# Eight matmul widths cut to three in TensorE's program of a routed expert layer

## The chip, the cores and the metric

The kernel runs on one core of a Trainium2 chip. The metric is the device time of one execution in microseconds (us), from the first to the last instruction and the little that lies around them. Lower is better.

## The reference, cut to what matters

```python
x = x + xattn(layernorm(x), ctx, W_k, b_k, gamma, beta)   # 4 x 1024 rows of 1024
xf = layernorm(x).reshape(4096, 1024)
probs = softmax(xf @ gate_w)                              # 8 experts
topk_w, topk_idx = top_k(probs, 2); topk_w /= topk_w.sum(-1)
# each row goes to its two experts; rows are sorted by expert:
h = silu(ragged_dot(rows, w1, sizes)) * ragged_dot(rows, w3, sizes)   # 1024 -> 3584
out = ragged_dot(h, w2, sizes)                                        # 3584 -> 1024
x = x + sum over the two experts of topk_w * out
```

All of it is float32. 8192 pairs of a row and an expert are spread over 8 experts, so an expert has about 1024 rows. How many is known only when the kernel runs.

## The kernel before, in words

A first part (the function `attend_and_route`, some 590 us) does the attention and the routing and leaves, for each expert, a list of its rows. Then `experts` works through slots. A slot is one expert with up to 1088 of its rows; this input fills eight slots, here called slot 0 to slot 7, one for each expert.

In a slot the rows lie in two halves side by side, so a matmul's moving side has as many columns as half the rows of the slot. That number, rounded up to one of the entries of `WIDTHS`, is the width of the slot. TensorE (PE) multiplies in the seven products of a Strassen scheme instead of eight, and each float32 operand is split into a high and a low part, so every product takes three matmuls for each k.

A slot has two stages. In the unit stage a unit is seven products of one weight (w1 or w3) for a pair of tiles of the hidden dimension: 28 units, each of 7 x 4 x 3 = 84 matmuls, or 168 where the width is over 512 and each matmul is cut in two. In the down stage there are seven passes over w2, each of five groups of steps, 168 matmuls (or 336) to a pass. Between the passes PE transposes: the rows of the next slot (`turn_rows`, L1789) or results on their way out (`turn_back`, L1808). ScalarE (ACT) makes the high parts of the weights and of the hidden rows, VectorE (DVE) the low parts and the sums (L1333 and L1336), and both empty PSUM. SyncE (SP) issues the loads of weights and the stores and loads of the hidden rows, which go through memory in `hd`. GpSimd (POOL) adds the results to the output by indirect DMA (`scatter`), and with `stage_pair` it loads w2 for sums (`stage`, the tiles `w2v` and `xg_0`).

All engines loop over the slots. ACT and DVE have three copies of a slot's code, for widths up to 512, 528 and 544. PE's loop over the units (L1824) and its loop over the groups (L1835) contain one body for every entry of `WIDTHS`; `by_width` (L1765) writes a binary search of compares and branches (L1772) around them, which is gone through again for each unit and each group. The bodies stand in the program from the widest to the narrowest. The engine's instructions are fetched from memory while it runs; the profile counts these fetches as packets of the queue q8 (16 KB each) and q14 (8 KB each).

In a unit PE waits at product 3 for ACT's copy of product 0's result (`s_s1`), at product 4 for DVE's sum u2 (`s_u2`, L1434), and at product 6 for DVE's c22 (`s_c22`, L1451). Ahead of c22, DVE has `down_sum(s, i, 0)` (L1450), which waits for the w2 that POOL's `stage_pair` loads:

```python
                if a == 0:
                    dve.wait_ge(s_sst, pr * 16 + 16)
                    down_sum(s, i, 0)
                plus(in_sbuf(to[:, 3], cols), in_sbuf(v, cols), in_psum(b4, cols)).then_inc(s_c22, 1)
```

In the down stage each group begins with `ready` (L1719), a wait for the low parts of w2 and of the hidden rows. The first of these hidden rows are loaded again only after SP has stored the last pair of the unit stage.

Of the kernel before, what the change touches and what calls it, by code (L numbers as in the profile page):

```python
# [61 lines left out]
SLOTS = 2 * T // (2 * HALF) + E - 1  # L62
META = 16
META_STEPS = 44
WIDTHS = (256, 384, 448, 480, 496, 512, 528, 544)
COLS = WIDTHS[-1]
TAIL = COLS - 4 * P
N8_MOST = COLS // 8
# [64 lines left out]
def attend_and_route(nc, x, ctx_in, W_k, b_k, gamma, beta, gate_w, x1_out, x2_rows, table, meta, first_weights):  # L133


    with ExitStack() as st:
# [440 lines left out]
        def _(dve):  # L577
# [175 lines left out]
            def by_slot(a):  # L753
# [30 lines left out]
            step(V.tensor_copy(metaf[:, 3, :], im[:, 1, :]))  # L784
            step(V.scalar_tensor_tensor(out=metaf[:, 2, :], in0=metaf[:, 3, :], scalar=float(WIDTHS[0] // 8),
                                        in1=has, op0=ALU.max, op1=ALU.mult))
# [85 lines left out]
def experts(nc, w1, w3, w2, out, x2_rows, table, meta, raw13, s_raw13):  # L872

    with ExitStack() as st:
# [229 lines left out]
        def _(act):  # L1104
# [179 lines left out]
            def slot(s, cols):  # L1284

                with act.Fori(0, PAIRS - 1) as i:
                    silu(free_at_start[:, 15:16], free_at_start[:, 14:15])
                    unit(s, i, 0, cols, lambda e: weight_hi(s, i, 1, e))
                    unit(s, i, 1, cols, lambda e: weight_hi(s, i + 1, 0, e))
                i = PAIRS - 1  # L1290
                silu(free_at_start[:, 15:16], free_at_start[:, 14:15])
                unit(s, i, 0, cols, lambda e: weight_hi(s, i, 1, e))

                def begin_down(e):
                    if e < 2:
                        w2_hi(s, e)
                    elif e in (3, 4):
                        h_hi(s, e - 3, cols)

                unit(s, i, 1, cols, begin_down)  # L1300
                down_phase(s, cols)
# [13 lines left out]
            with act.Fori(0, SLOTS) as s:  # L1315
                width = slot_value(act, 2, s, N8_MOST)
                with act.If(width > 0):
                    with act.If(width > BANK // 8):
                        with act.If(width > WIDTHS[-2] // 8):
                            slot(s, WIDTHS[-1])  # L1320
                        with act.Else():
                            slot(s, WIDTHS[-2])
                        act.nop()
# [5 lines left out]
        def _(dve):  # L1329
# [281 lines left out]
            def slot(s, cols):  # L1611

                with dve.Fori(0, PAIRS - 1) as i:
                    unit(s, i, 0, cols, lambda e: weight_lo(s, i, 1, e), lambda n: weight_sum(s, i, 1, n))
                    unit(s, i, 1, cols, lambda e: weight_lo(s, i + 1, 0, e), lambda n: weight_sum(s, i + 1, 0, n))
                i = PAIRS - 1
                unit(s, i, 0, cols, lambda e: weight_lo(s, i, 1, e), lambda n: weight_sum(s, i, 1, n))

                def begin_down(e):
                    if e < 2:  # L1620
                        w2_lo(s, e)
                    elif e in (3, 4):
                        h_lo(s, e - 3, cols)

                unit(s, i, 1, cols, begin_down, lambda n: None)
                down_phase(s, cols)
# [35 lines left out]
            with dve.Fori(0, SLOTS) as s:  # L1662
                width = slot_value(dve, 2, s, N8_MOST)
                with dve.If(width > 0):
                    with dve.If(width > BANK // 8):
                        with dve.If(width > WIDTHS[-2] // 8):
                            slot(s, WIDTHS[-1])
# [393 lines left out]
```

## Time and profile before

| what | value |
|---|---|
| time, three runs | 7847.52, 7869.36, 7878.46 us (median 7869.36) |
| time of the profiled execution | 7854.22 us |
| its span | 7852.5 us |
| PE busy | 7385.4 us, 94% of the span |
| DVE busy | 5046.7 us, 64% |
| ACT busy | 2873.4 us, 37% |
| POOL busy | 906.6 us, 12% |
| DMA | 159 GB/s over the span |
| granted clock of TensorE, mean | 0.97 |

The span is the time from the first to the last instruction. PE is busy nearly throughout, and 94% is a mean: in the middle of a unit stage it never stops, and between the stages it stands still for some microseconds. The chain of work that ended last has 85% of the span in PE, 3% in "issue" (an engine waited for nothing that the profile shows), 2% in DVE and 2% in DMA.

### The profile page before, as it was taken

What the parts mean: (1) busy time and instruction counts of PE and PEld (TensorE: products, weight loads), DVE (VectorE), ACT (ScalarE), POOL (GpSimd) and SP (SyncE); (2) the same over time, 40 slices, a digit from 0 to 9 for tenths busy, and PEclk for the clock granted to TensorE, in tenths of its full rate; (3) what the DMA queues carried; (4) which work ended last, traced back from release to release, by engine and by line L of the source; (5) the groups of instructions that cost most, each with busy time, mean ns of one, the idle gap of its engine ahead of it and who ended that gap; (6) DMA issues with size and microseconds to landing.
All of it is one profiled execution on the core that took longest, in us unless ns stands there. A gap on an engine that the chain in (4) does not pass through costs nothing.

```text
span 7852.5 us, 139132 instructions
## 1 busy us (share of the span) xinstructions
PE 7385.4 (94%) x45405; PEld 6600.8 (84%) x45406; DVE 5046.7 (64%) x8017; ACT 2873.4 (37%) x4875; POOL 906.6 (12%) x1344
## 2 busy tenths in 40 slices
PE   8959999899999999899999999999999999999998
PEld 5547877788779999888778999878778999999998
DVE  6767766577556665577556665577655665566655
ACT  2323334333443334333343333433343333433343
POOL 2330010100110010100010001100111001110011
PEclk8979999999999999999999999999999999999999
DMA  3333446544664445544564445544564445644455
GB/s 118 107 106 132 166 163 193 164 160 164 192 186 140 147 154 180 155 156 156 175 189 140 155 142 184 174 147 157 175 188 155 149 149 167 187 142 148 150 181 162
DMA packets 683970, 1247.95 MB, mean 159 GB/s; under 512 B 50528, under 2 KB 286448, under 8 KB 683632
## 3 DMA queue, kind: packets, MB, share of 16 engines
q1 hardware_dynamic: 584240, 935.24, 36.3%
q0 software_dynamic: 99392, 309.05, 12.2%
q8 instruction: 109, 1.79, 0.1%
q14 instruction: 229, 1.88, 0.1%
HBM read 840.81 MB, written 405.38 MB: 159 GB/s over the span
## 4 chain that ended last, share of the span: by engine, by line
PE 85%; issue 3%; DVE 2%; DMA 2%; ACT 0%; POOL 0%; SPq 0%; DVEq 0%; POOLq 0%; ACTq 0%
PE pair L1693 56%; PE pair L1726 27%; PE pair L1808 1%; DVE wl L1333 1%; DMA raw<-hd 1%; DMA raw<-in_L_ffn_w 1%; DVE sil L1336 0%; DVE hid L1336 0%; PE pair L1789 0%; DVE sil L1554 0%; ACT wh L1106 0%; DVE sil L1333 0%; POOL out_x L1926 0%; DVE xl L1333 0%; DVE hid L1424 0%
## 5 line engine op out<-in xcount | busy, mean ns | idle before, releaser
L1693 PE MATMUL pair<-xh,wh 128*128 128x264 f32 (+3 forms) x9408 | 2520.7, 322 | 100.5 <-issue 76.6
L1693 PE MATMUL pair<-xh,wl 128*128 128x264 f32 (+3 forms) x9408 | 2521.4, 323 | 12.9 <-issue 12.9
L1693 PE MATMUL pair<-xl,wh 128*128 128x264 f32 (+3 forms) x9408 | 2516.4, 322 | 0.0
L1333 DVE TENSOR_TENSOR wl<-raw,wh 128x512 fp32r<-128x512 f32 (+2 forms) x1875 | 1260.9, 692 | 1030.6 <-ACT wh L1106 1028.3
L1693 PEld LDWEIGHTS pair<-xh,wh 128*128 128x128 f32 x9408 | 1582.2, 190 | 240.7 <-issue 115.3
L1693 PEld LDWEIGHTS pair<-xh,wl 128*128 128x128 f32 x9408 | 1576.9, 189 | 141.7 <-issue 13.9
L1693 PEld LDWEIGHTS pair<-xl,wh 128*128 128x128 f32 x9408 | 1577.2, 189 | 122.4
L1106 ACT ACTIVATE wh<-raw 128x512 fp32r<-128x512 f32 (+2 forms) x1875 | 1136.9, 628 | 1351.3 <-PE pair L1693 611.8
L1726 PE MATMUL pair<-wh 128*128 128x264 f32 (+3 forms) x4704 | 1141.6, 326 | 144.4 <-issue 77.4
L1726 PE MATMUL pair<-wh,wl 128*128 128x264 f32 (+3 forms) x4704 | 1264.8, 323 | 0.0
L1726 PE MATMUL pair<-wl,wh 128*128 128x264 f32 (+3 forms) x4704 | 1264.5, 323 | 0.0
L1106 ACT ACTIVATE wh<-sums 128x512 fp32r<-128x512 f32 x900 | 566.3, 631 | 1545.2 <-PE pair L1693 1517.3
L1726 PEld LDWEIGHTS pair<-wh 128*128 128x128 f32 x4704 | 762.4, 191 | 231.7 <-issue 115.6
L1889 POOL TENSOR_TENSOR ticks<-ticks 128x1 f32<-128x1 f32 x316 | 115.9, 367 | 6333.5 <-DVE xg L1333 3276.3
L1726 PEld LDWEIGHTS pair<-wl,wh 128*128 128x128 f32 x4704 | 794.3, 191 | 62.8
L1726 PEld LDWEIGHTS pair<-wh,wl 128*128 128x128 f32 x4704 | 793.4, 191 | 63.1
L1333 DVE TENSOR_TENSOR wl<-sums,wh 128x512 fp32r<-128x512 f32 x900 | 616.8, 687 | 203.1 <-ACT wh L1106 195.0
L1336 DVE TENSOR_TENSOR part<-part,pair 128x512 f32<-128x512 f32 (+2 forms) x448 | 312.7, 698 | 469.6 <-PE pair L1693 469.6
L1333 DVE TENSOR_TENSOR wl<-part,wh 128x512 fp32r<-128x512 f32 (+1 forms) x272 | 186.5, 691 | 353.5 <-ACT wh L1106 353.1
L1106 ACT ACTIVATE wh<-part 128x512 fp32r<-128x512 f32 (+1 forms) x272 | 170.7, 630 | 421.1 <-PE pair L1726 397.8
L1109 ACT ACTIVATE sil<-sil 128x512 f32<-128x512 f32 (+2 forms) x336 | 215.5, 641 | 273.5 <-DVE sil L1336 262.3
L1336 DVE TENSOR_TENSOR sil<-part,pair 128x512 f32<-128x512 f32 (+2 forms) x368 | 254.8, 693 | 36.4 <-PE pair L1693 33.0
(253 smaller groups left out, 5473.4 us busy)
## 6 DMA issues: line engine op xcount, KB each, us to landing
raw<-in_L_ffn_w SPq DMA_DIRECT2D x226, 1024.0 KB, 7.8
raw<-hd SPq DMA_DIRECT2D x720, 272.0 KB, 3.6
hd<-hid SPq DMA_DIRECT2D x112, 1088.0 KB, 4.4
hd<-sil SPq DMA_DIRECT2D x112, 816.0 KB, 6.8
raw<-w2s SPq DMA_DIRECT2D x256, 256.0 KB, 3.3
w2v<-in_L_ffn_w POOLq DMA_DIRECT2D x112, 512.0 KB, 3.6
xg<-in_L_ffn_w POOLq DMA_DIRECT2D x112, 512.0 KB, 4.7
w2s<-w2v POOLq DMA_DIRECT2D x112, 512.0 KB, 5.2
```

What stands on the lines that cost most here:

```text
L1106: return nc.scalar.activation(out, in_, ACT.Copy)
L1109: return nc.scalar.activation(out, in_, ACT.Silu)
L1333: return V.tensor_tensor(out, a, b, ALU.subtract)
L1336: return V.tensor_tensor(out, a, b, ALU.add)
L1693: mm = pe.matmul(to[:, c, 0:hi - lo], entry(w, e)[:, ks], x[:, e, k, lo:hi], start=begin and k == 0 and i == 0, stop=k == KH - 1 and i == ...
L1726: mm = pe.matmul(pair[d][:, ch, 0:hi - lo], down_w(w, b)[:, d * P:(d + 1) * P], down_h(h, b)[:, lo:hi], start=begin, stop=end, skip_group_ ...
L1808: mm = pe.transpose(o, yT[:, d, j * P:j * P + r], ident[:, :])
L1889: G.tensor_tensor(ticks[:, 0:1], ticks[:, 0:1], ticks[:, 1:2], ALU.add).then_inc(s_tick, 1)
```

## The change

The list of widths loses five of its eight entries. The widest, 544, stays, and so do all sizes of buffers. What else is made from the list: the least value of a slot's stored width (L785, in eighths of a column, 32 before and 64 now), and PE's bodies and the search around them. A slot whose half has up to 512 columns now runs the body of 512; before, there were 256, 384, 448, 480 and 496 below it.

```diff
-WIDTHS = (256, 384, 448, 480, 496, 512, 528, 544)
+WIDTHS = (512, 528, 544)
```

PE's program has 1409 rows of different instructions before and 680 after. Those of DVE, ACT, POOL and SP are the same, in the same order.

At the head of the unit stage PE's order differs in the number of compares on the way to the first body in the program (the one of 544). The rows below are a piece of the difference; L1878 is the test for an empty slot, L1824 the entry of the loop over the units, L1698 and L1699 the first waits of a unit:

```order
 L1878 COMPARE_AND_BRANCH
 L1824 UNCONDITIONAL_BRANCH
-L1772 COMPARE_AND_BRANCH x3
+L1772 COMPARE_AND_BRANCH
 L1698 ISA
 L1699 ISA
```

The search has three levels before and one or two now; the first compare is against the same kind of register as before.

At the end of the loop over the units, just ahead of the down stage, PE's last body in the program before is that of 256 columns:

```order
L1693 MATMUL pair<-xh,wh 128x256
L1693 MATMUL pair<-xl,wh 128x256
L1693 MATMUL pair<-xh,wl 128x256
L1774 UNCONDITIONAL_BRANCH
L1824 REGISTER_ALU
L1824 COMPARE_AND_BRANCH
L1829 ISA
```

In the changed program the same place follows the body of 512 columns (`pair` is a PSUM tile, `xh` and `xl` the parts of the rows, `wh` and `wl` those of the weights):

```order
L1693 MATMUL pair<-xh,wh 128x512
L1693 MATMUL pair<-xl,wh 128x512
L1693 MATMUL pair<-xh,wl 128x512
L1774 UNCONDITIONAL_BRANCH
L1824 REGISTER_ALU
L1824 COMPARE_AND_BRANCH
L1829 ISA
```

Five bodies of 84 matmuls that stood between the body of 512 and the loop's end are gone, and the down stage, which follows, begins that much earlier in the program. In the loop over the groups five bodies of 40 matmuls are gone in the same way.

## Rows read from the trace of the kernel before

**Rows 1.** The page, its first line.
```profile
span 7852.5 us, 139132 instructions
```

**Rows 2.** Groups by line and form, L1693: count | busy us, mean ns | idle before.
```profile
L1693 PE MATMUL pair<-xh,wh 128*128 128x512 f32 x1568 | 620.3, 396 | 25.8 <-issue 21.3 <-DVE part L1336 2.6 <-ACT part L1106 1.8
L1693 PE MATMUL pair<-xh,wh 128*128 128x496 f32 x1568 | 613.0, 391 | 37.0 <-issue 17.9 <-DVE xl L1333 16.7 <-DVE wl L1333 2.4
```

**Rows 3.** The chain that ended last, in pieces: start us, us, what.
```profile
628.72 504.58 PE pair L1693 x2256
...
1331.04 38.01 PE pair L1726 x168
...
3298.32 524.19 PE pair L1693 x2256
...
4021.56 38.86 PE pair L1726 x168
```

**Rows 4.** Waits of PE from 600 us on: total us, times, longest us.
```profile
PE pair L1693 <- issue: 89.5, 17, 15.0
PE pair L1726 <- issue: 77.4, 25, 11.6
```

**Rows 5.** DMA queues, 1455 to 1500 and 5647 to 5702 us: packets, MB, share.
```profile
q8 instruction: 7, 0.11, 1.0%
...
q8 instruction: 5, 0.08, 0.5%
```

**Rows 6.** Timeline, turn from slot 5 to 6: start, us, instruction, [idle before].
```profile
5961.24 1.97 PE L1808 MATMUL pair<-ident,sil 128*128 128x128 f32 x16 [1.21 <-DVE sil L1336]
...
5969.81 0.58 PE L1693 MATMUL pair<-xh,wh 128*128 128x264 f32 x1 [6.61 <-issue]
...
5976.51 0.69 DVE L1333 TENSOR_TENSOR sums<-raw 128x512 f32<-128x512 f32 x1 [10.14 <-issue]
...
6001.10 0.80 PE L1693 MATMUL pair<-xh,wh 128*128 128x264 f32 x2 [3.34 <-issue]
```

**Rows 7.** Timeline, turn from slot 1 to slot 2.
```profile
2317.12 1.97 PE L1808 MATMUL pair<-ident,sil 128*128 128x128 f32 x16 [1.22 <-DVE sil L1336]
...
2342.64 0.69 DVE L1336 TENSOR_TENSOR xg<-w2v,xg 128x512 f32<-128x512 f32 x1 [1.15 <-DMA xg<-in_L_ffn_w]
...
2350.47 0.51 PE L1693 MATMUL pair<-xh,wh 128*128 128x272 f32 x2 [3.12 <-issue]
```

**Rows 8.** Chain in pieces, turns to slots 2 and 3, down stage of 3.
```profile
2344.10 3.28 PE pair L1693 x24
...
3285.48 10.20 PE pair L1693 x36
...
3844.55 0.69 DVE wl L1333
```

**Rows 9.** Timeline, turns to slot 3 and to slot 7.
```profile
3281.65 0.69 DVE L1333 TENSOR_TENSOR sums<-raw 128x512 f32<-128x512 f32 x1 [19.08 <-issue]
...
3298.32 0.49 PE L1693 MATMUL pair<-xh,wh 128*128 128x512 f32 x1 [2.67 <-issue]
...
6916.64 0.69 DVE L1333 TENSOR_TENSOR sums<-raw 128x512 f32<-128x512 f32 x1 [15.61 <-issue]
...
6935.02 0.66 PE L1693 MATMUL pair<-xh,wh 128*128 128x264 f32 x2 [2.88 <-issue]
```

**Rows 10.** Timeline of PE, start of the down stages of slots 3 and 5.
```profile
3826.93 1.09 PE L1789 MATMUL pair<-ident,xg 128*128 128x128 f32 x8 [1.64 <-DVE hid L1336]
...
3851.13 1.19 PE L1726 MATMUL pair<-wh 128*128 128x512 f32 x2 [11.42 <-issue]
...
3890.79 1.19 PE L1726 MATMUL pair<-wh 128*128 128x512 f32 x4 [1.13 <-DVE wl L1333]
...
5648.97 1.09 PE L1789 MATMUL pair<-ident,xg 128*128 128x128 f32 x8 [1.64 <-DVE hid L1336]
...
5701.69 1.19 PE L1726 MATMUL pair<-wh 128*128 128x512 f32 x4 [1.14 <-DVE wl L1333]
```

## The prediction, made before the changed kernel ran

> **What bounds the kernel now.** I read the page first: the span is 7852.5 us [rows 1], and PE is busy in 94% of it. Then the groups of matmuls kept apart by form, to learn which bodies this input uses. A slot issues 28 x 7 x 4 = 784 matmuls of xh with wh, so 1568 of 496 columns are two slots, and 1568 of 512 are two more [rows 2]. The other four slots run 528 (three) and 544 (one), in halves of 264 and 272. The bodies of 256, 384, 448 and 480 are never run. The chain in pieces tells which slots: 0 and 1 have 496 columns; 2 has 544; 3 and 5 have 512; 4, 6 and 7 have 528.
>
> So the change does two things to what runs. Slots 0 and 1 go from 496 to 512 columns, 16 more to each matmul, and those columns are waste. And PE's program gets about half as long, with one or two compares to find a body where there were three.
>
> In the middle of a unit stage PE is the bound without a gap. One piece of the chain holds 2256 matmuls in 504.58 us at 496 columns, another as many in 524.19 us at 512 [rows 3]. A compare costs nothing there, since PE's sequencer is ahead of its matmuls: I see no idle time at the seams of the units. The waits of PE show where it does stand: 89.5 us in 17 waits ahead of L1693 and 77.4 us in 25 waits ahead of L1726 that no semaphore explains [rows 4]. The timeline puts the long ones where PE goes from a slot's last transposes to the next slot's first unit, at the end of that first unit, and at the start of the down stage. Just there the queue q8 moves packets of 16 KB of instructions: 7 at the turn to slot 1, 5 at the start of the down stage of slot 5 [rows 5]. From 640 to 1130 us, 26 units long, the same view has no row for q8 at all. So PE keeps what a loop uses and fetches again when it goes to another part of the program.
>
> **The change, term by term.**
>
> *Columns.* 524.19 - 504.58 = 19.6 us for 2256 matmuls, 8.7 ns each [rows 3]. A slot's unit stage has 2352: +20.4 us, for two slots +40.8. A pass of the down stage takes 38.01 us at 496 and 38.86 at 512 [rows 3]: 0.85 x 7 = 6.0 a slot as the upper end. Some passes at 496 wait for DVE's halves, which hides part of it, so the lower end is nothing; I take 3.5 a slot. Sum of the columns: +47.8 us, from 40.8 to 52.8.
>
> *How much fits.* PE's code for a slot holds, before, 6 x 84 + 2 x 168 = 840 matmuls in unit bodies, 6 x 40 + 2 x 80 = 400 in group bodies and about 105 transposes, each with its weight load: 2690 instructions, with waits and branches some 3050. This code costs 7 + 5 = 12 packets in a slot [rows 5], so a packet is about 256 instructions. After the change it is 420 + 200 + 105 = 725 matmuls, 1450 instructions, some 1610 in all: 6.4 packets, so 7, and one more that is fetched ahead. Whether PE keeps 8 is the open point. The rows show that it keeps the 5 or 6 that the loop over the passes needs and does not keep 12. Eight is nearer to six than to twelve, so I take it that 8 fit; then PE fetches its slot code once, in slot 0, and never again.
>
> The Trainium skill bears on this (Runtime: NRT & Kernel Launch, Instruction fetch mechanics): PE's instruction memory is 128 KiB in blocks of 16 KiB, which makes 8 blocks and 2048 instructions. By it the sum stays as I make it, with all 8 places taken and none to spare. The same section says that a taken branch to a target outside a window of two pages forces a fetch. By that sentence alone nothing would be saved, as in rival 2. The trace speaks against it: each unit of 496 columns jumps over several bodies, and no packet moves.
>
> *What is late next at a turn.* Without the fetch PE would start the next slot within a microsecond of its last transposes. But ACT and DVE enter their own new code, which doesn't change, and POOL still has to scatter. Turn to slot 6: the transposes end at 5963.2, PE starts at 5969.8, DVE at 5976.5, and the second unit starts at 6001.1, 37.9 us after the transposes [rows 6]. Turn to slot 2, where PE's fetch was short: DVE has to wait for POOL's load of w2 until 2342.64, 23.55 us after the transposes [rows 7]; then comes c22, product 6 starts at 2344.10 and lasts 3.28 us [rows 8]. That is the floor, 28.3 us after the transposes, and after it come 3.1 us of fetch at the loop's end. So slot 2 gains 3.1 us. Slots 1, 4 and 6 look alike (within 1 us of it now, DVE in time); they fall to 28 each: 37.9 - 28 = 10, three times, -30 us.
>
> Where DVE is late it is the floor. At slot 3 it starts at 3281.65 [rows 9], and PE's product 4 starts 3.83 us after that; three products take 10.20 us [rows 8], though 36 x 0.232 = 8.4 at full rate: PE comes back slow from a stall. Only the fetch of 2.67 us at the end goes. At slot 7: 6916.64 + 3.8 + 10.6 = 6931.0 where 6935.02 is now [rows 9]: -4.0. Slot 5 is like slot 3, and I count 1. Sum of the turns: -3.1 - 30 - 2.7 - 4.0 - 1 = -40.8 us. If all idle time put to issue went, it would be far more (rival 3).
>
> *Start of the down stage.* In slot 3 the first transposes start at 3826.93 and pass 1 at 3890.79, 63.9 us; in slot 5, of the same width, 52.7 us [rows 10]. The difference is one gap of 11.4 us in slot 3. The low part that it needs began at 3844.55 and took 0.7 [rows 8]; PE went on at 3851.13 [rows 10], 5.9 later. So between 5.9 and 11.2 us go, and I take 8.5. Slot 0 has the same gap (11.6, the longest in [rows 4]): -17 us for both, from -11.8 to -22.4. In the other slots the gap ends with DVE's low part, so PE would only wait longer for that: nothing. If that cover were gone, they could share what else of the 77.4 us [rows 4] lies there.
>
> *Sum.* 47.8 - 40.8 - 17 = -10 us. The profiled execution took 7854.2, 15 below the median of the three runs; all four average 7862.4. Against its own time the sum is 7844; against the average, which I take, 7852.
>
> **The rivals.**
>
> 1. *It isn't 8 that fit.* The next page is fetched ahead, and with 7 places a ring of 8 pages misses on every one. Then 8 packets move in a slot where 12 did; half of the turns' gain is lost (20), and in slots 0 and 3 half of theirs (9): 7862 + 48 - 20 - 9 = 7881. For it: the rows show no case with exactly 8 in use. 17%.
>
> 2. *Nothing is saved, and the columns are paid* (the slower side). If each jump to a part not just run fetches again, or if the turns are bound by ACT, DVE and POOL more tightly than I read, the change is the columns alone: 7862 + 48 = 7910, +0.6%. That is also what the Trainium skill's sentence on taken branches (same page and section as above) would give, and the packets at rest in the loops don't bear it out. It decides once less than 9 us of the 58 are saved. For it: DVE is idle 10 to 19 us at the turns, so it comes late whatever PE does. Against it: at slots 1, 4 and 6 PE's second unit starts 9 us after the floor that slot 2 shows. 11%.
>
> 3. *The floors give way.* PE's fetches share the DMA engines with those of the other engines and with loads; without them DVE and ACT could enter earlier, and PE wouldn't fall to the slow rate. If 110 of the 166.9 us put to issue [rows 4] went, 7862 + 48 - 110 = 7800. Against it: POOL's scatter and load stand between, and they take 23.5 us at each turn. 12%.
>
> My forecast, a sum within some 20 us of -10: 60%.
>
> **How the numbers follow.** A measurement of this kernel can tell about 0.5% from no change, 39 us. The likeliest case lies inside it: 7852, its own range 7830 to 7875. Rival 1 is inside it too. Rival 2 is at the edge of slower: I give slower 12%. Faster takes rival 3 and a little of the forecast's lower side: 17%. Same: 71%. The range leaves out rival 3's far end and most of rival 2's: 7818 to 7892.
>
> **What the profile after would show.** In the view of DMA queues q8 has no packets between slot 0's first down pass and the kernel's end. The units of slots 0 and 1 run 512 columns, their pieces of the chain 524 us. At the turns to slots 1, 4 and 6 the second unit starts 28 to 29 us after the transposes, and PE's waits there are for DVE or ACT and no longer for issue. The gap of 11.4 us in the down stage of slot 3 is about 5. Wrong would be: q8 still moving at each turn (rival 1 or 2), a second unit that starts less than 25 us after the transposes (rival 3), or a piece of 2256 matmuls in slot 0 that isn't 524 us.

## The result, and the profile after

The changed kernel takes 7806.7 us (median of 4 runs, 7795.73 to 7812.29) where the kernel before, run beside it, takes 7868.62 (7847.52 to 7878.46). The ratio is 0.993, with a 95% interval of 0.9912 to 0.9947: 0.7% faster. The forecast was 7852, with 7818 to 7892 around it. The measured time lies 11 us below the bottom of that range. The profiled execution took 7804.17 us, 50 less than that of before (7854.22), where my sum said 10 less.

The page of the changed kernel, its first line, PE's granted clock in 40 slices, and the queue that brings PE's instructions (packets, MB, share):

```profile
span 7802.5 us, 138313 instructions
...
PEclk9979999999999999999999999999999999999999
...
q8 instruction: 14, 0.23, 0.0%
```

The same row of the kernel before:

```profile
q8 instruction: 109, 1.79, 0.1%
```

So 95 of 109 instruction packets are gone. In the view of DMA queues restricted to 1250 to 7802 us, q8 has no row at all: after slot 0's first down pass no packet of q8 moves. That is the test that I had set for "8 pages fit".

The groups by line and form, which answer to [rows 2], and a piece of the chain that ended last, which answers to [rows 3] (start us, us, what). Four slots now have 512 columns, 3136 = 4 x 784, and 2340 matmuls of slot 0 in 545.34 us are 0.2330 us each, as 524.19 / 2256 = 0.2324 before:

```profile
L1693 PE MATMUL pair<-xh,wh 128*128 128x512 f32 x3136 | 1237.1, 394 | 44.1 <-DVE xl L1333 17.0 <-ACT part L1106 15.0 <-DVE part L1336 7.4
```

```profile
610.00 545.34 PE pair L1693 x2340
```

The waits of PE from 600 us on, which answer to [rows 4]. The row L1693 <- issue (89.5 us before) isn't there any more, and L1726 <- issue is down from 77.4 to 25.6. Some of it has turned into waits for DVE and ACT:

```profile
PE pair L1726 <- DVE wl L1333: 58.0, 34, 4.9
...
PE pair L1726 <- issue: 25.6, 10, 2.9
PE pair L1693 <- ACT part L1106: 20.5, 5, 10.7
...
PE pair L1693 <- DVE part L1336: 15.8, 6, 4.6
```

The timeline at the turn from slot 5 to slot 6, which answers to [rows 6]. PE starts 1.3 us after its last transposes where it stood 6.6 before, then waits for ACT and DVE in pieces; the second unit starts at 5969.77, 29.0 us after the transposes (37.9 before):

```profile
5938.80 1.97 PE L1808 MATMUL pair<-ident,sil 128*128 128x128 f32 x16 [1.21 <-DVE sil L1336]
...
5942.05 0.50 PE L1693 MATMUL pair<-xh,wh 128*128 128x264 f32 x2 [1.28 <-DVE hid L1554]
...
5952.39 0.50 PE L1693 MATMUL pair<-xh,wh 128*128 128x264 f32 x2 [1.22 <-ACT part L1106]
...
5958.19 0.50 PE L1693 MATMUL pair<-xh,wh 128*128 128x264 f32 x2 [2.62 <-DVE part L1336]
```

The timeline of PE at the start of the down stage of slot 3, which answers to the first half of [rows 10]. The longest gap was 11.42 us and is 4.87 now, and pass 1 starts 50.2 us after the start of the transposes where it took 63.9. The two gaps aren't the same wait, as the next part shows:

```profile
3837.84 1.09 PE L1789 MATMUL pair<-ident,xg 128*128 128x128 f32 x8 [1.64 <-DVE hid L1336]
...
3853.38 0.80 PE L1726 MATMUL pair<-wh 128*128 128x512 f32 x1 [4.87 <-DVE wl L1333]
...
3888.07 1.19 PE L1726 MATMUL pair<-wh 128*128 128x512 f32 x4 [1.10 <-DVE wl L1333]
```

**Where the 50 us went.** I divided both executions at the same points of PE's timeline in each slot: the end of the last transposes before it, the start of its second unit, the end of its last unit, the start of pass 1 of its down stage (the second of its seven passes). Sums over the eight slots, in us:

| stretch | before | after | change | forecast |
|---|---|---|---|---|
| prologue, to the first unit's data | 587.9 | 593.0 | +5.1 | 0 |
| turns (transposes to second unit) | 296.4 | 254.0 | -42.4 | -40.8 |
| 27 units, slots 0 and 1 | 1016.1 | 1053.7 | +37.6 | +39.3 |
| 27 units, other slots | 3306.6 | 3296.5 | -10.1 | 0 |
| down starts (last unit to pass 1) | 473.4 | 426.7 | -46.7 | -17 |
| passes 1 to 6 | 2144.0 | 2150.8 | +6.8 | +7 |

(The forecast's column term, +47.8, is spread over the rows where it falls; 1.5 of it lies in the first units.) Slot by slot the down starts are:

| slot | 0 | 1 | 2 | 3 | 4 | 5 | 6 | 7 |
|---|---|---|---|---|---|---|---|---|
| before | 65.1 | 54.8 | 57.5 | 65.5 | 58.4 | 54.4 | 58.8 | 59.0 |
| after | 53.1 | 52.1 | 55.2 | 51.9 | 54.3 | 52.0 | 53.4 | 54.7 |
| forecast, change | -8.5 | 0 | 0 | -8.5 | 0 | 0 | 0 | 0 |

Two rows miss: the down starts by 30 us and the units of the other slots by 10. The stretches of "passes 1 to 6" include the transposes between and behind them; what is left, some 28 us behind the last slot, is the same in both.

**What the trace shows there.** A down start is made of steps: twelve matmuls (24 where each is cut in two) on one tile of w2 and one of hidden rows, so DVE makes two low parts for each. Slot 7 shows best what PE waited for, since there the low parts of hidden rows are 528 wide and those of w2 512. DVE before, from the end of the units (7491.53) on; the low parts of the first two steps are made earlier, so the rows are those of the third step, and then the first and second of the fourth:

```profile
7499.14 0.69 DVE L1333 TENSOR_TENSOR wl<-part,wh 128x512 fp32r<-128x512 f32 x1 [4.62 <-ACT wh L1106]
7499.75 0.70 DVE L1333 TENSOR_TENSOR wl<-raw,wh 128x528 fp32r<-128x528 f32 x1
...
7508.54 0.69 DVE L1333 TENSOR_TENSOR wl<-raw,wh 128x512 fp32r<-128x512 f32 x1 [7.48 <-ACT wh L1106]
7510.41 0.71 DVE L1333 TENSOR_TENSOR wl<-raw,wh 128x528 fp32r<-128x528 f32 x1 [1.18 <-ACT wh L1106]
```

PE before, at its third step, and the q8 row of the view of DMA queues from 7500 to 7512 us:

```profile
7509.66 2.10 PE L1726 MATMUL pair<-wh 128*128 128x264 f32 x8 [8.34 <-DVE wl L1333]
```

```profile
q8 instruction: 3, 0.05, 2.5%
```

The profile puts the 8.34 us to DVE, since a low part of DVE had ended last. But both low parts of the third step were done at 7500.45, before the gap began (7501.32), and PE went on before the hidden rows' low part of the fourth step had begun. So the gap wasn't for DVE. Three packets of q8 moved around it, and it is gone in the changed kernel: it was a wait for code. In all seven slots that have such a gap the low parts were done 0.6 to 0.9 us before it began; the profile puts it to DVE in slots 1, 5, 6 and 7 and to issue in 0, 3 and 4. The gaps of 11.64 and 11.42 us in slots 0 and 3 stand at the same place, in front of the third step. PE's gaps of each slot in front of its third and its fourth step, in us (0: none):

| slot | 0 | 1 | 2 | 3 | 4 | 5 | 6 | 7 |
|---|---|---|---|---|---|---|---|---|
| third step, before | 11.64 | 3.70 | 0 | 11.42 | 7.81 | 2.59 | 8.10 | 8.34 |
| third step, after | 0 | 0 | 0 | 0 | 0 | 0 | 0 | 0 |
| fourth step, before | 0 | 0 | 5.61 | 0 | 0 | 0 | 0 | 0 |
| fourth step, after | 3.19 | 4.93 | 4.17 | 4.87 | 4.61 | 4.84 | 4.34 | 4.59 |

What stops PE now is the fourth step's hidden rows, which come back from memory. ACT, DVE and PE of slot 7 after (the units end at 7445.09):

```profile
7460.55 0.64 ACT L1106 ACTIVATE wh<-raw 128x528 fp32r<-128x528 f32 x1 [1.67 <-DMA raw<-hd]
```

```profile
7461.23 0.71 DVE L1333 TENSOR_TENSOR wl<-raw,wh 128x528 fp32r<-128x528 f32 x1 [1.62 <-ACT wh L1106]
```

```profile
7462.31 0.81 PE L1726 MATMUL pair<-wh 128*128 128x264 f32 x2 [4.59 <-DVE wl L1333]
```

So the fourth step starts 17.0 to 17.3 us after the units in slots 1 to 7 (18.1 in slot 0), and before it started 18.6 to 31.1 us after them. This also bounds the gain: slot 7 lost a wait of 8.34 us and gained 4.3.

Slot 5 gained 2.3 us. PE before, then PE after; the units ended at 5647.34 before and at 5627.37 after:

```profile
5653.97 1.19 PE L1726 MATMUL pair<-wh 128*128 128x512 f32 x4 [3.04 <-issue]
...
5657.36 0.63 PE L1726 MATMUL pair<-wl,wh 128*128 128x512 f32 x1
5657.79 0.63 PE L1726 MATMUL pair<-wh,wl 128*128 128x512 f32 x1
...
5663.97 1.17 PE L1726 MATMUL pair<-wh 128*128 128x512 f32 x4 [2.59 <-DVE wl L1333]
```

```profile
5632.15 0.39 PE L1726 MATMUL pair<-wl,wh 128*128 128x512 f32 x1
5632.38 0.39 PE L1726 MATMUL pair<-wh,wl 128*128 128x512 f32 x1
...
5644.49 0.50 PE L1726 MATMUL pair<-wh 128*128 128x512 f32 x1 [4.84 <-DVE wl L1333]
```

The last wait ends 16.6 us after the units before and 17.1 after them now, but 24 matmuls were done by then and now 36. The idle time itself fell by only 0.8 us: 3.04 and 2.59 went, 4.84 came. The rest is PE's speed. After the stall of 3.04 us the matmuls start 0.43 us apart; without that stall, 0.23. The windows show the clock and count the matmuls (PE busy with count, PEld busy with count, PEclk, DMA share, GB/s; L1726 alone). Before, then after:

```profile
5653.00:5662.00 9.00, 7.40 (x24) 5.57 (x24) 0.81 1.03 354
```

```profile
5630.00:5642.00 12.00, 8.93 (x36) 6.63 (x36) 1.00 0.91 324
```

The granted clock is 0.81 over the nine microseconds behind the stall for code, so PE spends part of them at 1.2 GHz and not 2.4; after, it is 1.00. Over all eight down starts PE's idle time fell by 37.4 us (96.9 to 59.5) and the time in which it ran by 9.3 (376.5 to 367.2), although slots 0 and 1 have 16 columns more to a matmul.

A part of the waits for data moves with PE as well. The ACT rows of slot 5, before and then after, are the high part of the third step's w2:

```profile
5658.54 0.63 ACT L1106 ACTIVATE wh<-part 128x512 fp32r<-128x512 f32 x1 [6.81 <-PE pair L1726]
```

```profile
5634.24 0.63 ACT L1106 ACTIVATE wh<-part 128x512 fp32r<-128x512 f32 x1 [2.49 <-PE pair L1726]
```

ACT waits for PE to free the weights: 11.2 us after the units before, 6.9 after them now. The hidden rows of the fourth step don't move by as much; and in slot 2, where no wait for code stood in front of a step, its fourth step started 1.4 us earlier too, which no run explains.

The units of the other slots gain in the same way. At slot 2 the loop's end cost 3.12 us [rows 7], and in the windows of all engines (PE, PEld, DVE, ACT, POOL busy with counts, PEclk, DMA share, GB/s) the granted clock falls just behind it, where the second unit has begun:

```profile
2347.30:2350.40 3.10, 0.06 (x1) 0.00 (x0) 2.56 (x4) 1.29 (x2) 0.72 (x2) 1.00 0.16 32
2350.40:2353.80 3.40, 3.33 (x17) 3.33 (x18) 0.00 (x0) 0.00 (x0) 0.87 (x2) 0.60 1.04 351
2353.80:2358.00 4.20, 4.20 (x32) 4.20 (x32) 1.29 (x2) 1.14 (x2) 0.19 (x1) 0.91 0.48 195
```

3.4 x 0.40 + 4.2 x 0.09 = 1.7 us, and slot 2's 27 units did take 570.1 before and 568.4 after. It holds slot by slot. In the first 12 us of the second unit the granted clock of slots 0 to 7 was 1.00, 0.86, 0.86, 1.00, 0.76, 0.86, 0.76 and 0.86 before, a loss of 0, 1.7, 1.7, 0, 2.9, 1.7, 2.9 and 1.7 us, and 1.00 in all of them after. The 27 units of slots 2 to 7 got shorter by 1.7, 0.1, 2.6, 1.7, 2.5 and 1.6 us, and those of slot 1 grew by 1.6 us less than slot 0's.

### The profile page after: what moved, and what is told of

The parts are those of the page before. It is cut to its first block, busy times and chain, and to the rows that moved or that the text cites. A ratio compares the mean times of both kernels' runs of the same rounds, so it can differ in the third digit from the quotient of the medians.

```text
span 7802.5 us, 138313 instructions
## 1 busy us (share of the span) xinstructions
PE 7413.9 (95%) x45405; PEld 6576.3 (84%) x45406; DVE 5045.2 (65%) x8017; ACT 2872.3 (37%) x4875; POOL 911.5 (12%) x1344
## 4 chain that ended last, share of the span: by engine, by line
PE 85%; issue 2%; DVE 2%; DMA 2%; ACT 0%; POOL 0%; SPq 0%; DVEq 0%; POOLq 0%; ACTq 0%
PE pair L1693 56%; PE pair L1726 27%; DMA raw<-hd 1%; PE pair L1808 1%; DVE wl L1333 1%; DVE sil L1336 0%; DVE hid L1336 0%; POOL out_x L1926 0%; DVE sil L1554 0%; PE pair L1789 0%; DVE sil L1333 0%; ACT wh L1106 0%; DVE hid L1424 0%; DVE xl L1333 0%; DMA xg<-in_L_ffn_w 0%
## 5 line engine op out<-in xcount | busy, mean ns | idle before, releaser
L1693 PE MATMUL pair<-xh,wh 128*128 128x264 f32 (+2 forms) x9408 | 2522.0, 322 | 68.7 <-ACT part L1106 20.5
L1693 PE MATMUL pair<-xh,wl 128*128 128x264 f32 (+2 forms) x9408 | 2532.6, 324 | 0.0
L1693 PE MATMUL pair<-xl,wh 128*128 128x264 f32 (+2 forms) x9408 | 2528.9, 323 | 0.0
L1333 DVE TENSOR_TENSOR wl<-raw,wh 128x512 fp32r<-128x512 f32 (+2 forms) x1875 | 1261.0, 692 | 979.2 <-ACT wh L1106 977.0
L1693 PEld LDWEIGHTS pair<-xh,wh 128*128 128x128 f32 x9408 | 1577.6, 189 | 224.8 <-issue 83.9
L1693 PEld LDWEIGHTS pair<-xl,wh 128*128 128x128 f32 x9408 | 1573.4, 189 | 138.2
L1693 PEld LDWEIGHTS pair<-xh,wl 128*128 128x128 f32 x9408 | 1572.6, 189 | 138.0
L1726 PE MATMUL pair<-wh,wl 128*128 128x264 f32 (+2 forms) x4704 | 1265.6, 323 | 0.0
L1726 PE MATMUL pair<-wl,wh 128*128 128x264 f32 (+2 forms) x4704 | 1264.1, 323 | 0.0
L1726 PE MATMUL pair<-wh 128*128 128x264 f32 (+2 forms) x4704 | 1142.4, 326 | 103.9 <-DVE wl L1333 58.0
L1726 PEld LDWEIGHTS pair<-wh 128*128 128x128 f32 x4704 | 759.1, 190 | 194.3 <-issue 96.4
L1726 PEld LDWEIGHTS pair<-wl,wh 128*128 128x128 f32 x4704 | 791.4, 190 | 65.9
L1726 PEld LDWEIGHTS pair<-wh,wl 128*128 128x128 f32 x4704 | 791.0, 190 | 66.4
L1333 DVE TENSOR_TENSOR wl<-sums,wh 128x512 fp32r<-128x512 f32 x900 | 616.7, 687 | 210.4 <-ACT wh L1106 205.5
L1333 DVE TENSOR_TENSOR wl<-part,wh 128x512 fp32r<-128x512 f32 (+1 forms) x272 | 186.5, 691 | 304.1 <-ACT wh L1106 303.6
L1336 DVE TENSOR_TENSOR sil<-part,pair 128x512 f32<-128x512 f32 (+2 forms) x368 | 254.8, 693 | 41.7 <-PE pair L1693 41.4
```

The source lines that it names most:

```text
L1333: return V.tensor_tensor(out, a, b, ALU.subtract)
L1336: return V.tensor_tensor(out, a, b, ALU.add)
L1693: mm = pe.matmul(to[:, c, 0:hi - lo], entry(w, e)[:, ks], x[:, e, k, lo:hi], start=begin and k == 0 and i == 0, stop=k == KH - 1 and i == ...
L1726: mm = pe.matmul(pair[d][:, ch, 0:hi - lo], down_w(w, b)[:, d * P:(d + 1) * P], down_h(h, b)[:, lo:hi], start=begin, stop=end, skip_group_ ...
```

## The experiments

Twelve kernels, each compared with the kernel before, run on the same chip beside it. That kernel took 7849 to 7851 us there, and 7869 beside the changed one, so the ratios are compared (the changed kernel's is 0.993), and the microseconds of an expectation are read as differences. The theory: PE's instruction pages (the packets of q8, by my estimate 256 instructions each) explain the stalls, and each stall costs once more by the lower clock behind it. The edits are shown against the changed kernel, but for the last two.

**1. Eight bodies, none under 512 columns run.** The columns alone, with the old size of program.

```
-WIDTHS = (512, 528, 544)
+WIDTHS = (256, 384, 448, 480, 496, 512, 528, 544)
...
-  scalar=float(WIDTHS[0] // 8),     (least width of a slot, L785)
+  scalar=float(64),
```

> All eight bodies stay in the program, but no slot is narrower than 512, so slots 0 and 1 run the same bodies as in the changed kernel: the columns alone, with the old size of program. Theory (the columns cost what the two traces show, +19.6 and +18.0 us for 27 units and about +5 in the down passes, and everything else came from the program's size): 36 to 48 us over the kernel before, near 7910, instruction fetches about as many as before (109), and the turns at 37 to 39 us in slots 1, 4 and 6 as before. Rival (the extra columns partly hide waits for VectorE and ScalarE, so the size of the program brought less than it seems): within 20 us of before, near 7880.

Measured: 7893.33 us beside 7851.31, ratio 1.0055 (1.0037 to 1.0072), so 42 us more. q8 moved 104 packets, and PE's waits for issue are back:

```profile
PE pair L1726 <- issue: 97.6, 23, 13.8
PE pair L1693 <- issue: 80.0, 16, 9.5
```

The turns of slots 4 and 6 took 37.6 and 37.7 us; slot 1's took 34.7, less than I had said. The units of slots 0, 1 and 3 took 528.5, and 526.8 in the changed kernel, which has the same columns. So the columns cost 42 us (14 us either way by the interval), and the smaller program gave 1.0055 - 0.993 = 1.25%, 98 us.

**2 and 5. Bodies that no slot runs.** One more body, then two more, with the least width kept at 512.

```
-WIDTHS = (512, 528, 544)
+WIDTHS = (384, 512, 528, 544)          (2)
+WIDTHS = (256, 384, 512, 528, 544)     (5)
```

> The changed kernel with a fourth body (384) that no slot ever runs: size and position of the code alone, same columns, same work. Theory (the gain is that TensorE's code of a stage stays in its instruction memory, and it takes 8 pages of 256 instructions, the next one fetched ahead): slots 0 to 3 as in the changed kernel, refetches come back where slots of 528 and 512 alternate (slots 4, 6 and 7), 25 to 45 fetches in all in place of 14, and 15 to 40 us over the changed kernel, 7820 to 7848. Rival 1 (it is the number of compares before a body, at most two here as in the changed kernel): equal to the changed kernel, 7807 within 8. Rival 2 (anything over three bodies loses it all): all of the 100 us that the size brought are gone, about 7905.

> The changed kernel with two more bodies (256 and 384) that no slot runs. One dead body cost 8 us beside a fourth of the refetches of before. Theory (pages: with five bodies the code of a stage no longer fits, whether the bodies are run or not): 70 to 95 instruction fetches, the turns back near 37 us in slots 1, 4 and 6 and the down starts at 54 us or more, 20 to 50 us over the changed kernel, ratio to the kernel before 0.9965 to 1.0000. Rival (only bodies that are run count): as with one dead body, 0.993 to 0.995.

Measured: 7804.65 us, 0.9947 (0.9933 to 0.9961), and 7842.47 us, 0.9989 (0.998 to 0.9998). The rows of q8 with one body more, and with two:

```profile
q8 instruction: 45, 0.74, 0.0%
```

```profile
q8 instruction: 69, 1.13, 0.1%
```

Nothing that runs has changed, and 14 packets became 45 and 69, the three ratios 0.993, 0.9947 and 0.9989. One dead body is cheaper than I had said: it has 31 more packets, the turns grew by 11.5 us (254.0 to 265.5) and the down starts by 1, and its ratio is within the other's interval (0.17% more, 13 us, if it is taken as it is). In the down starts the waits for code are back in front of the third step of slots 4, 6 and 7 (5.32, 4.87 and 3.74 us), but there they take the place of the wait for hidden rows behind it. Two cost about 0.6%, 46 us; the turns took 270.4, the down starts 443.8. In slots 1 and 2 the turns were still 29.9 and 28.1 there, so pages come back slot by slot and not all at once. The time with one body alone would not have excluded the rival that compares are the cost (it said 7807 within 8). The rival that only bodies that run count has fallen; so has the one that compares are the cost, since a slot of 512 or 528 columns passes two compares with three, four and five bodies alike.

**3. Four bodies that all run.** Slots 0 and 1 get their 496 columns back.

```
-WIDTHS = (512, 528, 544)
+WIDTHS = (496, 512, 528, 544)
```

> Four bodies (496, 512, 528, 544), so slots 0 and 1 run at 496 columns as in the kernel before: the columns are given back and the program is one body larger than the changed one. Theory (columns and size add): the 27 units of slots 0 and 1 back at 507 to 509 us each, 40 to 46 us off the changed kernel, and 15 to 40 us back for refetches in slots 4, 6 and 7, so 7780 to 7805. Rival (compares, not size): 7765. Rival (four bodies lose all that the size brought): about 7865.

Measured: 7758.14 us, 0.988 (0.9865 to 0.9895): 0.5% under the changed kernel. 27 units of slots 0 and 1 took 507.1 us each, the turns 259.8 in all, the down starts 426.0; q8 moved 45 packets as in experiment 2. It came out below the bottom of the theory's range, since refetching cost 5 us and not the 15 to 40 that I had written. The 39 us less are nearest to the rival's number (7765, 42 us less); what speaks against that rival is experiment 5, and the packets. Columns and pages are separate terms that add: 42 us of columns against 5 of pages.

**4. Filling the waits.** The test of the clock by itself: unused matmuls where PE waits for other engines.

```
+def keep_busy(to, n):
+    for _ in range(n):
+        pe.matmul(to.rearrange("p (a b) -> p a b", a=4), ident[:, :],
+                  ident[:, :].unsqueeze(1).to_broadcast([P, 4, P]), start=True, stop=True,
+                  skip_group_check=True)
...
 turn_rows(xg, 1, read, s_xg, s * 128 + 32)
+keep_busy(pair[0][:, 0, :], 4)             (ahead of the down passes)
...
 turn_tail(s_acc[1], s * EVENTS + 4 + 2 * 2, s_xgt, s * 16 + 16)
+keep_busy(pair[0][:, 0, :], 2)             (ahead of pass 3)
 pe.wait_ge(s_tq, s + 2)
```

> The changed kernel with six matmuls a slot that compute nothing used (they write a bank that the next pass overwrites): four of 512 columns ahead of the first down pass, about 3.4 us, and two, about 1.7 us, ahead of the wait in front of pass 3. Each is shorter than the wait that follows (4.2 to 4.9 us, and 2.5 to 2.9), which is for other engines. Theory (after a wait of 2.5 us or more TensorE runs 3.4 us at the lower of its two clocks, and that was the other half of what each removed stall gave): the wait is shorter than 2 us, the granted clock stays at 1.00 behind it, and each place saves about 1.7 us, two places in eight slots, 15 to 27 us off the changed kernel, 7780 to 7792. Rival (the lower clock is not set by the wait, or the waits move on with the added work): no change or up to 20 us more, 7807 to 7827.

Measured: 7775.84 us, 0.9902 (0.9889 to 0.9915), against 0.993: 22 us less, in the range. PE at the down start of slot 5:

```profile
5608.53 3.60 PE L1825 MATMUL pair<-ident 128*128 128x512 f32 x8
...
5622.15 0.51 PE L1726 MATMUL pair<-wh 128*128 128x512 f32 x1 [1.73 <-DVE wl L1333]
```

and the windows around that wait:

```profile
5617.50:5622.00 4.50, 2.91 (x13) 2.06 (x11) 1.68 (x4) 2.21 (x5) 0.00 (x0) 1.00 1.04 401
5622.00:5625.60 3.60, 3.45 (x15) 2.84 (x16) 3.60 (x7) 2.46 (x6) 0.00 (x0) 1.00 0.63 209
```

The same two windows in the changed kernel, without the fill:

```profile
5639.60:5644.40 4.80, 0.05 (x1) 0.00 (x0) 1.67 (x3) 2.27 (x5) 0.00 (x0) 1.00 1.03 402
5644.40:5648.00 3.60, 3.51 (x9) 2.82 (x10) 3.60 (x7) 2.11 (x5) 0.00 (x0) 0.57 0.63 191
```

The wait ends 17.05 us after the units, as it did without the fill (17.12), so the data came no earlier; PE ran faster behind it. 3.6 us of useless work took 1.6 us off the down start (52.0 to 50.5). (The row counts two records for each of the four matmuls.) In the eight slots the down starts fell from 426.7 to 412.7 and passes 1 to 6 from 2150.8 to 2134.3: 14.0 and 16.5 us. More work and less time, with no page moved (14 packets) and the data no earlier: the clock behind the wait gave it, 1.00 in place of 0.57. Experiments 11 and 12 bear it out for pass 3 with the code in the same place.

**6 and 7. A fill at the turn, and all three.** Four unused matmuls at the end of each slot, alone and with those of experiment 4.

```
                     (end of the loop over p)
+keep_busy(pair[3][:, 1, :], 4)
```

> The changed kernel with four matmuls of 512 columns that compute nothing used at the end of each slot (3.4 us), ahead of the next slot's first unit; the first unit waits 3.5 to 10.8 us for VectorE and ScalarE in slots 1 to 7 anyway. Theory (the lower clock after a wait costs as much as a part of the wait, and the wait ends at a time set by other engines): where one wait of 3.5 to 4.6 us stands alone (slots 1, 2 and 4) it falls under 1.5 us and the granted clock stays at 1.00 behind it, 1.5 to 3 us saved a slot; where 7 us or more are waited in pieces (slots 3, 5, 6 and 7) the lower clock stays in one of them and 0 to 3 us are saved; after the last slot nothing waits for TensorE, 0 to 3 us lost. In all 6 to 18 us off the changed kernel, ratio to before 0.9905 to 0.9925. Rival (the waits are for data whose time goes by TensorE's own progress): 15 to 28 us more.

> The changed kernel with all three fills: four unused matmuls ahead of each slot's first down pass, two ahead of the wait in front of pass 3, and four at the end of each slot. Theory: the gains add, 20 us (measured for the first two) and 6 to 18 for the third, ratio to before 0.988 to 0.9895. Rival (the fill at the turn only moves the wait): as with the first two alone or worse, 0.990 to 0.993.

Measured: 7795.75 us, 0.9939 (0.9925 to 0.9952), and 7775.64 us, 0.9908 (0.9893 to 0.9923). The theory missed: at the turns the fill brought nothing, alone or with the others. The turns sum to 254.8 us and 256.4, where it was 254.0. At the turn to slot 1 PE had one wait of 4.61 us in its first unit; now it has two:

```profile
1482.33 0.49 PE L1693 MATMUL pair<-xh,wh 128*128 128x512 f32 x1 [2.79 <-DVE part L1336]
...
1491.35 0.60 PE L1693 MATMUL pair<-xh,wh 128*128 128x512 f32 x1 [3.19 <-DVE sil L1336]
```

The wait moved on and split, which is the rival of experiment 7. The data that the first unit waits for isn't due at one time, as it is at the down start.

**8, 9 and 10. Four bodies with fills.** With all three, with the short one alone, and with the two at the down passes.

```
-WIDTHS = (512, 528, 544)
+WIDTHS = (496, 512, 528, 544)
+keep_busy(pair[0][:, 0, :], 4)     ahead of the down passes    (8, 10)
+keep_busy(pair[0][:, 0, :], 2)     ahead of pass 3             (8, 9, 10)
+keep_busy(pair[3][:, 1, :], 4)     at the end of the slot      (8)
```

> Four bodies (496, 512, 528, 544) and all three fills together, the version that the runs point to. Theory (columns, pages and the lower clock are separate terms that add): 0.988 for the four bodies, 20 us less for the fills at the down passes and 6 to 18 for the one at the turn, ratio 0.983 to 0.985. Rival (with four bodies the instruction fetches return in slots 4, 6 and 7, the fill ahead of the down passes meets a wait for code and not for data there, and is paid in full): 0.986 to 0.989.

> Four bodies (496, 512, 528, 544) and only the short fill, two unused matmuls ahead of the wait in front of pass 3, where no slot fetches code. With all three fills the down starts of slots 4, 6 and 7 were 2 to 3.5 us longer than without any, and 1.7 us shorter elsewhere. Theory (a fill pays where its wait is for data and costs where the wait is for code): 8 times 1.7, 14 us off the four bodies alone (0.988), ratio to before 0.9855 to 0.987. Rival (with fetches in the program the waits there are not the same): 0.988.

> Four bodies, with the fills ahead of the first down pass and ahead of pass 3, none at the turn (the fill at the turn brought nothing measured). Theory: five slots gain 1.7 us at the down start and three lose 2 to 3.5, so within 4 us of the version with the short fill alone, ratio 0.9855 to 0.9875. Rival (what was lost in the version with all fills came from the fill at the turn, which made the program longer): 0.9835 to 0.9855.

Measured: 7748.91 us, 0.9868 (0.9853 to 0.9883); 7752.64 us, 0.987 (0.9847 to 0.9893); 7737.31 us, 0.9855 (0.9836 to 0.9875). The first is the rival of experiment 8. The down start of slot 4 took 57.1 us there, and 53.6 without fills, since the wait behind the fill, in front of the third step, was for code (the changed kernel has none there). It is as long behind the fill as in experiment 3 without it (3.64 us), so the fill was paid in full:

```profile
4688.54 3.60 PE L1825 MATMUL pair<-ident 128*128 128x512 f32 x8
...
4701.54 2.10 PE L1726 MATMUL pair<-wh 128*128 128x264 f32 x8 [3.58 <-DVE wl L1333]
```

The short fill alone took passes 1 to 6 from 2140.0 to 2126.5 us, 1.7 us a slot, but its ratio can't be told from that of four bodies alone. The third is the fastest kernel of this study: 113 us, 1.45%, under the one before. Its ratio stands on the border between the two expectations, so whether the fill at the turn did harm in experiment 8 isn't settled.

**11 and 12. The kernel before with the same fills, and with their place alone.** Eight bodies; in experiment 12 each added matmul has 8 columns in place of 512.

```
+pe.matmul(to[:, 0:8], ident[:, :], ident[:, 0:8], start=True, stop=True, skip_group_check=True)   (12)
```

> The kernel before, eight bodies, with the two fills at the down passes. In the changed kernel they gave 20 us in the medians. Theory (a stall for code can't be filled by code that comes ahead of it, and the wait for data behind it is already shorter, 0 to 2.6 us; the wait in front of pass 3 is the same 2.9 us as in the changed kernel): the short fill saves 1.7 us in each slot, 14 us, the long one saves nothing and costs 0 to 3.4 us a slot, so from 14 us less to 14 us more, ratio 0.998 to 1.002. Rival (the lower clock costs as much whatever the wait was for, and fills help in the same way): 0.997 or less.

> The kernel before with the same twelve instructions at the same places as in the version that fills it, but each added matmul has 8 columns in place of 512, so the code lies the same and almost no time is filled. With the fills the long stall for code in the down starts of slots 0 and 3 (11.4 us each) was gone, which neither theory had said. Theory A (the position of the code decides whether pages push each other out twice there): the stall is gone here too, down starts of slots 0 and 3 at 54 to 58 us, about 20 us off the kernel before, less nothing for pass 3, ratio 0.996 to 0.999. Theory B (the fill gave the fetches the time in which they ran ahead): the down starts of slots 0 and 3 stay at 63 to 66 us, ratio 0.999 to 1.002. In both, pass 3's start keeps its wait of 2.9 us or less and the lower clock behind it, so the later passes stay where they were, 2144 us in all and not 2130.

Measured: 7820.67 us, 0.996 (0.9947 to 0.9973), and 7832.78 us, 0.9979 (0.9969 to 0.999). Experiment 11 gave more than the theory said (0.998 to 1.002); its ratio is one that the rival had named (0.997 or less), but the stretches show another cause. Passes 1 to 6 fell by 13.8 us (2144.0 to 2130.2), 1.7 a slot as in experiment 4. But the down starts of slots 0 and 3 fell from 65.1 and 65.5 to 54.2 and 55.8, while those of the other slots stood (343 to 344 us in sum). Experiment 12 says what did it. With almost nothing filled, they are 54.7 and 56.0, and passes 1 to 6 take 2146.2: 16 us more than in experiment 11, whose code lies the same. PE at slot 3's down start there, to be laid beside the 11.42 of [rows 10]:

```profile
3823.77 1.56 PE L1726 MATMUL pair<-wh 128*128 128x512 f32 x4 [3.17 <-issue]
...
3834.41 1.87 PE L1726 MATMUL pair<-wh 128*128 128x512 f32 x4 [3.27 <-issue]
```

q8 moved 99 packets in both experiments and 109 before; from the end of slot 3's units to its third step's start 4 moved, where 7 had. So the long stall hung on where the code lies in its pages: a shift by a dozen instructions brought 11.42 us down to 3.27 and took 17 us off the whole. Why there are fewer packets then, the runs don't show.

## Why the prediction was wrong, step by step

**Which bodies run, and the columns: right.** Forecast +47.8, from 40.8 to 52.8. Experiment 1 gives +42. In the traces, slot 0's 27 units grew by 19.6 us, as worked out from [rows 3]; the six passes behind gave 5.0 in slots 0 and 1 together.

**Eight pages fit: right.** q8 is silent from 1250 us on. One body more, run or not, and packets move again. The runs show that some 1610 instructions (my estimate, 7 packets) are kept and that one body more isn't kept whole; that an eighth place is taken by a page fetched ahead they don't show by itself. This also fits the Trainium skill's 8 blocks of 16 KiB (Runtime: NRT & Kernel Launch, Instruction fetch mechanics). Its sentence there, that a taken branch out of a window of two pages forces a fetch, isn't what this trace shows: PE jumps through all of a slot's code, seven turns long, without a packet. Rivals 1 and 2 have fallen.

**What is late next at a turn: right.** Forecast -40.8, measured -42.4. By slot, 0 to 7, the forecast was 0, -10, -3.1, -2.7, -10, -1, -10 and -4.0 and the traces give -2.6, -10.4, -2.2, -4.2, -8.8, -1.3, -8.9 and -4.1; that the sum is so near owes something to chance, slot 0's above all. In slots 1, 4 and 6 the second unit starts 28.4, 28.9 and 29.0 us after the transposes, as I had said (28 to 29), and PE waits there for ACT and DVE. The floors held, so rival 3, whose 7800 us is nearest to what was measured, was right in its number and wrong in its place. One of its clauses was right in part, that PE wouldn't fall to the slow rate: behind the loop's end it doesn't any more, behind the waits for data it still does (0.57 in slot 5).

**The start of the down stage: this step failed.** It said -17 us, 8.5 in slots 0 and 3, and "In the other slots the gap ends with DVE's low part, so PE would only wait longer for that: nothing." Measured -46.7: 25.7 in slots 0 and 3, and 21 in the other six. What failed is the reading of that wait. The row [2.59 <-DVE wl L1333] of slot 5 names the low part that ended last, which is one of the fourth step; PE stood in front of its third, whose low parts were done at 5660.49, before PE stopped (5661.38). In slots 1, 4, 5, 6 and 7 this gap (3.70, 7.81, 2.59, 8.10 and 8.34 us) was for code, as in slots 0 and 3, and all of it went. What the change runs into is another wait, the one for the hidden rows of the fourth step, 17.0 to 17.3 us after the units. The prediction took a wait for code as a wait for data, and so it never looked for the data that would be late. Slot 3's range has the same fault: the low part that began at 3844.55 is of the fifth step, those of the third were done at 3839.00, before the gap began (3839.71), so the lower end of 5.9 us had no ground. That the gap of slot 3 is "about 5" now, as I had said, is luck: the gap of 11.4 us is gone, and the 4.87 us are the wait for the hidden rows.

And a stall costs more than its gap. Behind it the granted clock is at 1.2 GHz for part of the next microseconds; of the 46.7 us, 9.3 are time in which PE ran and 37.4 idle time. Experiment 4 shows the clock's share by itself, 1.6 to 2 us at each place. I had seen the slow rate at slot 3 (10.20 us for 36 matmuls) and used it there to explain a duration, and had not asked what the same rate costs behind each of the 42 waits put to issue.

In slots 0 and 3, -12.1 and -13.6 stand against 8.5 each (upper bound 11.2). Experiment 12, which removes most of the long stall alone, gives 10.4 and 9.5 of it; the rest, 1.6 and 4.1, is like the 2.3 to 5.4 us of the other slots.

**Units of the other slots: put at nothing without a reason.** 10 us came from the clock behind the wait at the loop's end, a wait that I had priced by its gap alone (3.1 us in slot 2).

The rest, +5.1 us in the prologue, is hardly the change's: in the other runs the same point lies between 584.4 and 591.2 us, and at 585.9, 588.5 and 589.8 in the three that also have three bodies. The medians differ by 62 us where the profiled executions differ by 50; I can't divide that.

**What stays open.** Why the long stall sits in slots 0 and 3 before, in 1 and 3 in experiment 1, in 0 alone in experiment 5, and in none in experiments 11 and 12 was not settled beyond its hanging on position. Nor does a run explain why the hidden rows of the fourth step are ready earlier after the units now, 1.3 to 2.9 us in slots 1 to 7, beyond the part of the copies that wait for PE. And at the turns it wasn't tried to place a fill inside the first unit, where its second wait is.

## What to carry to other kernels

Before costing a wait at nothing because another engine ends it, count the matmuls up to it and find the operands that just this step needs: if they were there before the wait began, the engine named isn't its cause. Then look for the next operand that will be late, since that one bounds the gain. Price a stall as its gap and what the granted clock loses behind it, and where a wait for data of known length can't be removed, work that isn't needed can pay for itself, but not where the wait is for code. A width that saves columns and a body that costs pages are separate terms: here four bodies with refetches beat three without.

## What the runs showed of the chip that I had not expected

- 3.6 us of unused matmuls ahead of a wait of 4.84 us made the kernel faster: the wait fell to 1.73 us, and the granted clock behind it was 1.00 in place of 0.57.
- PE kept all of its slot code, by my estimate 7 packets of 256 instructions, through seven slots without a packet. With one body more, 31 more packets moved and the turns grew by 11.5 us, but the down starts by 1 only: waits for code of 3.7 to 5.3 us there took the place of waits for data. (That the spans are alike, 7801.7 and 7802.5 us, is chance: passes, units and prologue were 13 us shorter in that execution, with the same work.)
- Six small matmuls and their weight loads, put ahead of two stretches of the down stage, turned a stall of 11.4 us into one of 2.3 to 3.3 in two slots, with eight bodies in the program.
- The 27 units of a slot of 528 columns take 554.9 or 559.7 us in the same kernel, with no waits in them: after, slots 4 and 6 took 559.7 and slot 7 554.9; with a dead fourth body it was the other way round. It is 5 us a slot that no run explains.
